# A graph kernel on one core: VectorE's first one-hots of a bucket wait for less, and TensorE's transposes and product change places

## The reference

```python
agg = segment_sum(h[src], dst, N)
z = relu(((1 + eps_gin) * h + agg) @ W1 + b1) @ W2 + b2
z = (z - mean(z, 0)) * rsqrt(var(z, 0) + 1e-5) * gamma + beta
x1 = layernorm(x + (z + h))            # h is x
support = segment_sum(edge_weight[:, None] * x1[dst], src, N)
out = layernorm(x1 + relu(support @ weight))
```

## Time and profile before

| | |
|---|---|
| time, median of 3 runs | 5424.88 us (5422.3 to 5427.39) |
| profiled execution, span of its instructions | 5351.1 us |
| difference, taken as what lies around the span | 73.8 us |
| PE busy | 3721.5 us, 70% |
| PEld busy | 3045.6 us, 57% |
| POOL busy | 3177.6 us, 59% |
| DVE busy | 2301.2 us, 43% |
| ACT busy | 1495.5 us, 28% |

### The profile page before, as it was taken

The page is one execution under the profiler, slowest core; times in us unless marked ns, Lnnn a source line. Parts: engine busy times, 40 slices in busy tenths (PEclk is TensorE's granted clock), DMA queues, the critical chain, the costliest instruction groups (busy, mean ns, idle before and its releaser), DMA issues.

```text
span 5351.1 us, 79415 instructions
## 1 busy us (share of the span) xinstructions
PE 3721.5 (70%) x16131; PEld 3045.6 (57%) x16132; DVE 2301.2 (43%) x5448; ACT 1495.5 (28%) x4377; POOL 3177.6 (59%) x3352
## 2 busy tenths in 40 slices
PE   2677676667667776767742667777777777777777
PEld 2565555555555655656632556566665666665666
DVE  2545454545555544545563233333333333333333
ACT  2444444445444444444552000000000000000001
POOL 6666655565656665666335666666666666666662
PEclk6887888888887878888855789888888888888898
DMA  4333333333333333333293333333333333333331
GB/s 134 93 97 92 99 90 97 90 97 93 95 93 97 93 97 91 96 97 99 62 298 123 90 94 99 96 101 96 100 101 99 95 100 100 102 97 97 100 100 53
DMA packets 298112, 541.14 MB, mean 101 GB/s; under 512 B 77802, under 2 KB 190302, under 8 KB 297838
## 3 DMA queue, kind: packets, MB, share of 16 engines
q0 software_dynamic: 159424, 434.52, 28.3%
q10 hardware_dynamic: 89348, 67.77, 4.0%
q1 hardware_dynamic: 49066, 36.39, 2.2%
HBM read 489.80 MB, written 46.88 MB: 100 GB/s over the span
## 4 chain that ended last, share of the span: by engine, by line
issue 27%; ACTq 16%; another core or an unknown queue 15%; PE 15%; ACT 12%; DVE 9%; DVEq 4%; DMA 2%; SPq 1%; POOL 0%; PEldq 0%; POOLq 0%
PE ps L1419 10%; ACT ones_sb L1613 7%; DVE work L1096 7%; ACTq L1611 4%; ACTq L1613 2%; DVEq L1096 2%; PE ps L1221 2%; ACT ring L1611 2%; ACTq L1642 1%; PE ps L1459 1%; ACT ones_sb L1619 1%; ACTq L1617 1%; ACTq L377 1%; PE ps L1292 1%
## 5 line engine op out<-in xcount | busy, mean ns | idle before, releaser
L548 POOL DMA_INDIRECT ring<-in_x,idx x1664 | 1587.9, 954 | 1039.5 <-issue 456.4
L606 POOL DMA_INDIRECT ring<-x_dram,idx x1612 | 1528.0, 948 | 904.9 <-issue 479.8
L1419 PE MATMUL ps<-ring,work 128*128 x6448 | 1631.3, 411 | 581.1 <-DVE work L1096 387.5
L1419 PEld LDWEIGHTS ps<-ring,work 128*128 128x128 f32 x6448 | 1327.7, 208 | 851.0 <-issue 649.4
L1221 PE MATMUL ps<-ring,ones_sb 128*128 x3708 | 1115.7, 449 | 454.8 <-ACT ones_sb L1619 301.9
L1096 DVE TENSOR_SCALAR work<-ps,dstT,wT 128x256 f32<-128x256 f32 x1612 | 748.0, 536 | 1551.6 <-remote 977.0
L1221 PEld LDWEIGHTS ps<-ring,ones_sb 128*128 128x128 f32 x3708 | 800.4, 225 | 676.6 <-issue 550.2
L1613 ACT ACTIVATE ones_sb<-tile_nodes,dstT 128x128 f32<-128x128 f32 x1854 | 651.0, 391 | 396.5 <-issue 331.1
L1292 PE MATMUL ps<-work 128*128 128x128 f32 x3384 | 499.2, 301 | 203.6 <-issue 148.1
L1292 PEld LDWEIGHTS ps<-work 128*128 128x128 f32 x3384 | 484.0, 216 | 233.5 <-issue 189.8
L1791 ACT ACTIVATE work<-ps 128x512 f32<-128x512 f32 x49 | 29.3, 597 | 1764.2 <-remote 1111.7
(11 more groups left out here) (240 smaller groups left out, 2299.3 us busy)
## 6 DMA issues: line engine op xcount, KB each, us to landing
ring<-in_x,idx POOLq DMA_INDIRECT x1664
ring<-x_dram,idx POOLq DMA_INDIRECT x1612
z_dram<-z_pair ACTq DMA_DIRECT2D x49, 256.0 KB
ones_sb<-x_dram ACTq DMA_DIRECT2D x49, 256.0 KB
ring<-z_dram SPq DMA_DIRECT2D x24, 512.0 KB, 4.1
ring<-in_x SPq DMA_DIRECT2D x24, 512.0 KB, 5.6
x_dram<-ring ACTq DMA_DIRECT2D x24, 512.0 KB
out<-ones_sb ACTq DMA_DIRECT2D x48, 256.0 KB
```

What stands on the lines that cost most here:

```text
L548: nc.gpsimd.indirect_dma_start(out=ring[:, q, c, :], out_offset=None, in_=x, in_offset=bass.IndirectOffsetOnAxis(ap=idx[:, q, c:c + 1], ax ...
L606: nc.gpsimd.indirect_dma_start(out=ring[:, q, c, :], out_offset=None, in_=x1_dram, in_offset=bass.IndirectOffsetOnAxis(ap=idx[:, q, c:c + ...
L1419: last = nc.tensor.matmul(to[:, t * D:(t + 1) * D], ones_of[:, b, c, t * P:(t + 1) * P], ring[:, ds((p + b) & (RING - 1), 1), c, :].rearra ...
```

## The change

- `table2` gets a sixth column, `PREV2`, and 16-bit integers in place of 32-bit ones. The column holds `head` of the bucket before (0 for the first), that is, where that bucket's loop part ends. Two table instructions more in `chunk_rows`.
- `steps2`: the bucket's first turn of four pairs leaves the loop. It waits once, until the loop part of the bucket before is done, and writes both groups. The loop begins with the third group, with the waits of before.
- TensorE: `turn2(j-1)` goes from behind head group 3 to behind group 1; `conv(j-2)` from behind groups 1 and 2 to behind groups 3 and 4. At the very end `turn2(NBK-1)` comes ahead of `conv(NBK-2)`.
- ScalarE: `turned2(i)` also waits until `conv(i-1)` is done (`s_conv`), since it overwrites `sumT`, which that product reads.
- `entry`, the first stage's loader, no longer has the argument that skips the check of bounds. `entry2` keeps it.

```diff
--- before.py
+++ after.py
@@ -153,7 +153,7 @@
         first_pair = sb("first_pair", [P, NB1], f32)
         batches_i = sb("batches_i", [1, 3, NBK], i32)
         rounds_i = sb("rounds_i", [1, 2], i32)
-        table2 = sb("table2", [1, NBK, 5], i32)
+        table2 = sb("table2", [1, NBK, 6], mybir.dt.uint16)
         work = sb("work", [P, WORK], f32)
         zero_row = sb("zero_row", [P, D], f32)
         all_ones = work[:, 3200:3200 + P]
@@ -375,8 +375,7 @@
         def entry(eng, j):
 
             _, values = nc.values_load_multi_w_load_instructions(
-                table[0:1, ds(j, 1), :].rearrange("a t f -> a (t f)"), engines=[eng.engine], min_val=0, max_val=MOST,
-                skip_runtime_bounds_check_because=IN_RANGE)
+                table[0:1, ds(j, 1), :].rearrange("a t f -> a (t f)"), engines=[eng.engine], min_val=0, max_val=MOST)
             return values
 
         def in_tiles(j):
@@ -403,7 +402,7 @@
 
 
         NEW, HEAD, M4, M2, END, OFF, COL, REP, PREV, MID = range(10)
-        NEW2, M42, HEAD2, M22, END2 = range(5)
+        NEW2, M42, HEAD2, M22, END2, PREV2 = range(6)
         MOST = PADP * NT
 
 
@@ -950,6 +949,8 @@
                 sync()
                 setup(nc.vector.tensor_scalar(batches_i[:, 2, :], batches_i[:, 1, :], TWO, None, ALU.bitwise_and))
                 setup(nc.vector.tensor_copy(table2[0:1, :, HEAD2], first_pair[0:1, 0:NBK]))
+                setup(nc.vector.memset(table2[0:1, 0:1, PREV2], 0))
+                setup(nc.vector.tensor_copy(table2[0:1, 1:NBK, PREV2], first_pair[0:1, 0:NBK - 1]))
                 sync()
                 setup(nc.vector.tensor_tensor(taken[0:1, 0:NBK], first_pair[0:1, 0:NBK], batches_i[:, 2, :], ALU.subtract))
                 sync()
@@ -1087,7 +1088,7 @@
             nc.vector.tensor_copy(into_f, key_i).then_inc(s_keys, 1)
 
             def steps2(j):
-                new, m4, head, m2, end = entry2(dve, j)
+                new, m4, head, m2, end, prev_head = entry2(dve, j)
 
                 def weighted(to, p, n):
                     at = nc.s_assert_within(p, 0, ROWS - n, skip_runtime_bounds_check_because=IN_RANGE2)
@@ -1098,7 +1099,12 @@
                     last.then_inc(s_onehot2, n)
 
                 with dve.If(new < m4):
-                    with dve.Fori(new, m4, 2 * TWO) as p:
+                    dve.wait_ge(s_added2, prev_head + RING)
+                    stand(dve)
+                    for b in range(0, 2 * TWO, TWO):
+                        weighted(loop2[:, b:b + TWO], new + b, TWO)
+                with dve.If(new + 2 * TWO < m4):
+                    with dve.Fori(new + 2 * TWO, m4, 2 * TWO) as p:
                         for b in range(0, 2 * TWO, TWO):
                             dve.wait_ge(s_added2, p + (b + RING - TWO))
                             weighted(loop2[:, b:b + TWO], p + b, TWO)
@@ -1406,7 +1412,7 @@
             pe.wait_ge(s_w3, 16)
 
             def sum_bucket(j, bank, others):
-                new, m4, head, m2, end = entry2(pe, j)
+                new, m4, head, m2, end, _ = entry2(pe, j)
                 to = acc2[bank]
                 nc.tensor.matmul(to, zeros[0:1, 0:P], zeros[0:1, :], start=True, stop=True)
 
@@ -1463,19 +1469,19 @@
             def bucket(j, bank, n):
 
                 def part_a():
+                    if n >= 1:
+                        turn2(j - 1)
+
+                def part_b():
+                    pass
+
+                def part_c():
                     if n >= 2:
                         conv(j - 2, [0])
 
-                def part_b():
+                def part_d():
                     if n >= 2:
                         conv(j - 2, [1])
-
-                def part_c():
-                    if n >= 1:
-                        turn2(j - 1)
-
-                def part_d():
-                    pass
 
                 sum_bucket(j, bank, [part_a, part_b, part_c, part_d])
 
@@ -1487,8 +1493,8 @@
                 bucket(2 * h + 1, 1, 2)
             if NBK % 2:
                 bucket(NBK - 1, 0, 2)
+            turn2(NBK - 1)
             conv(NBK - 2)
-            turn2(NBK - 1)
             conv(NBK - 1)
 
 
@@ -1788,6 +1794,9 @@
 
             def turned2(i):
                 act.wait_ge(s_sum2_turned, i + 1)
+                if not (isinstance(i, int) and i == 0):
+                    act.wait_ge(s_conv, i)
+                    stand(act)
                 nc.scalar.activation(sumT.rearrange("p t k n -> p t (k n)"), p_sumT[:, :, 0:D], ACT.Copy).then_inc(s_sum2T, 1)
 
             def deviations_v(i):
```

## The result

The changed kernel takes 5622.9 us (5617.7 to 5650.5, four runs) against 5423.6 of the kernel before (5411.4 to 5427.4, four runs): ratio 1.0389, interval 1.0355 to 1.0424. It is 199 us slower. The forecast was 78 us slower; the direction held, the size did not.

What follows compares the result with a forecast made beforehand. No engine was full; waits between engines bound both stages, above a gather floor. Check +265, earlier one-hots -127, later product -60 gave +78 on 5424.9: 5503 us, 1.4% slower, range 5,200 to 5,640.

Steps and rivals of the forecast that it cites:

- if the second stage gets shorter by under 60 us: Sign that the prediction is wrong; others: second stage shorter by over 300 us, first stage's end moving under 100 us.
- (4) The check: Stage one, table loader: ten checks a tile on TensorE and ScalarE, 2.7 us each tile, 265 us lost (0 to 470).
- TensorE's own checks hide behind ScalarE's in part: Stage one: TensorE stood 245.5 us for ScalarE, so its own checks were to cost less than their full time.
- the check costs nothing: Rival, stage one: checks not emitted or swallowed by the gap at the tile's start; 5238 us, chance 0.22.
- (1) Earlier one-hots: Stage two: wait ahead of a bucket's first groups goes, third group late next; 127 us gained (0 to 387.5).
- half lies ahead of the first group: Stage two: of TensorE's 387.5 us wait for one-hots, half ahead of the first group, from 22.5 of 43.8 us.
- (2) The product behind later groups: Stage two: product behind later head groups no longer waits for L1122's residual sum; 60 us gained (0 to 65).
- (3) ScalarE's wait: Stage two: copy of the transposed sums waits for the preceding bucket's product; costs nothing, at most 0.6 us a bucket.
- The lag is work: Rival, stage two: products still run after their recorded end, earlier one-hots save only 64 us; 5566 us, chance 0.13.
- slower than all this: Outcome slower than the forecast case's own range and the slower rival; chance 0.03.
- All waits go: Rival, stage two: third group's waits are echoes of lateness at the start, 447 us gained; 5243 us, chance 0.10.
- The 73.8 us that I took to lie around the span: Whole kernel: profiled span 5351.1 us against the timed median 5424.9; the difference was left unchanged in the forecast.

Runs made afterwards that it cites:

- check_only: Kernel before with the bounds check of the first stage's ten entries switched on and the second stage's table in 16 bits; 5673.0 us, 1.0421 of before.
- after_again: The changed kernel run again, unaltered, on the visit of the variants that take the change apart; 5659.3 us, 1.0395 of before.
- the ground: Comparison kernel, the same as base_u16: kernel before with both tables in unsigned 16-bit integers, check still skipped; 5467.7 us.
- no_gather2: base_u16 with the second stage's 1,612 row gathers left out and a semaphore raised instead (wrong sums); 4565.1 us, 0.8494 of before.
- reorder_only: base_u16 with TensorE's new order and ScalarE's new wait alone; 5392.6 us, 1.0006 of before.
- onehots_only: base_u16 with the earlier one-hots alone, TensorE's order and ScalarE as before; 5369.2 us, 0.9995 of before.
- stage2_only: Changed kernel without the check, first table in unsigned 16-bit integers, so stage two's edits alone; 5447.1 us, 1.0010 of before.
- check_pe: base_u16 with the check of the ten entries on TensorE's loads only; 5584.9 us, 1.0386 of before.
- base_u16: Kernel before with both tables in unsigned 16-bit integers, check still skipped; 5467.7 us, 1.0054 of before.

## Why the prediction was right or wrong

The sum was +265 for the check and -187 for stage two. In runs of one visit it is +231 (check_only against before) and -14 (after_again against check_only), 217 us; on the visit of the result it was 199. So the step that failed is the 187 us for stage two, waits of TensorE taken at their full length as time gained, and the prediction's own sign said so: "if the second stage gets shorter by under 60 us"; it got 18 us shorter than the ground's, or 6 us longer than before's.

**(4) The check: the mechanism right, the size near.** That ten checks are emitted, on both engines, 980 times each, was right, and so was that they lie in the open; stage one ends 222 to 268 us later, as forecast. I took 2.7 us a tile; it is 231/98 = 2.4 against before. The price is made otherwise than I had it. The load grew by 0.64 us, 63 us in 98 tiles, which I had left out. "TensorE's own checks hide behind ScalarE's in part" wasn't borne out: on TensorE alone they cost 2.0 us a tile. They stand at the head of a tile on TensorE's own sequencer; the 245.5 us of waits for ScalarE took up 3.0 us a tile, and came again in part as other pauses and as longer busy time at a lower granted clock. The chain in the earlier trace rows through ScalarE's load was read rightly, and the chain of the changed kernel runs there still. That the terms come so near 2.7 holds some luck: the load was missing, and the gaps between instructions were an estimate. The rival "the check costs nothing" (decides below 1.9 us a tile) falls on its size and on its reason.

**(1) Earlier one-hots: the step that failed.** The wait ahead of the first groups went and the third group was late next, as the step said; the wait fell even further, to 197.5 us over the stage, than the 260 forecast. Counted over all 49 buckets of the trace before, 99.5 us of the 387.5 stood ahead of the first group, 77.3 ahead of the second, 104.9 and 105.7 ahead of the third and fourth; in the changed kernel nothing, nothing, 146.7 and 48.3. So "half lies ahead of the first group", from four buckets, was a quarter, which the second group made up for. What failed is the price: I took a wait that goes for time that is gained. Its 127 us came to nothing measurable (0.9995), at most some 15 us, since pauses without a releaser took its place. The warning stood in my own rows: VectorE was idle in all four stalls and got the count 6 to 11 us late. I read that as a delay of a signal that could be run around. It is there only while gathers run (no_gather2), and that it meets TensorE wherever it stands is my reading of the two waits tables, not shown by itself.

**(2) The product behind later groups: the same error.** L1122's wait went from 65.4 us to 5.3:

```profile
  PE ps L1465: 5.3, 2
```

Its 60 us came to nothing (1.0006, 0.9985 to 1.0026). The wait went, and the stage didn't end earlier by it.

**(3) ScalarE's wait: nothing that shows.** It wasn't run by itself; reorder_only, which holds it together with (2), is within 0.1% of before. In the changed kernel the copy waits for the product as said (575.7 us, 17 times, idle time of ScalarE). One of the terms put at 0 isn't quite: TensorE's load of the six short entries takes 1.46 us a bucket and that of the five long ones took 1.24 (medians), 0.22 x 49 = 11 us if nothing hides it.

**The rivals.** "The lag is work" had the right side: earlier one-hots would give only 64 us. Its reason, products that still run, isn't shown; its sum, 5566, still credited 124 us to stage two, where 14 to 21 were measured. The measured 5622.9 us lies above the forecast case's own range (5,440 to 5,600) and above this rival, in what had got 0.03 as "slower than all this". "All waits go" (5243) is refuted by onehots_only, where half of them went for nothing. My test for it, that the gather floor leaves room, was only a necessary one.

**Span and median.** The 73.8 us that I took to lie around the span don't exist: the profiled execution of the changed kernel took 5617.7 us with a span of 5615.9, 1.8 us around it, and that of the ground 2.5. The profiled execution before was a short one; whether by chance or because it was of another visit isn't recorded. It did no harm to the sum, which is made of differences.

**What stays open.** What the pauses are, and why some visits don't have them; ScalarE's own share of the check where they are; whether stage two's edits are worth 20 us or nothing; why the loads of the table differ in length. None of the kernels with the reference's result beats the kernel before by more than its interval. The changed kernel's second stage without the check is stage2_only, which keeps the argument.

## What to carry to other kernels

A releaser's name on a wait tells who came last, not what the wait is worth: before pricing its removal, ask what that engine itself was late from, and if the lag has no work under it, let zero be the likely gain until a run shows more. Checks of values read to registers took their sequencer's time on each engine that read them, and at the head of a tile on TensorE they weren't hidden where TensorE set the pace, and were where gathers did. A variant that is to be the ground must be read in the trace like any other: here its tables' type alone made the load twice as long. And a part of a change that nobody meant, here an argument dropped from a helper, can outweigh the part that was meant.

## What the runs showed of the hardware

- Ten checked entries on TensorE alone make a tile 2.0 us longer (check_pe), though each register instruction is 0.147 us and each assertion 0.018 (medians).
- Loading ten table entries on TensorE's queue took 1.19 us from 32-bit signed integers without the check, 1.84 with it, and 2.39 from unsigned 16-bit ones without it (medians of 98 each: before, after, base_u16).
- One kernel takes 4,330 us on some visits and 5,400 on others, the chip numbered 5 among both. What marks the longer times goes when indirect gathers are left out: stage two then has, on a visit of 5,380 us, no register instruction of 0.70 us, next to no idle time without a releaser, and a granted clock of 1.00 (2.4 GHz) where before's was 0.86. The lower level (0.50, 1.2 GHz) stood there behind pauses of TensorE, as from 4,026 to 4,034 us, after 0.9 us of work in the 4 us before.
- On quick visits gathers of 128 rows are issued one each 1.25 us, at 256 bytes a row as at 1,024 (1,442 and 1,440 of them in 1,800 us).
- Longer pauses of TensorE came with a lower clock: with the check on TensorE its granted clock in stage one was 0.77, in kernels without it 0.82 to 0.84, and by the two windows 0.6 us a tile were longer busy time.
